# Value projections ahead of the loop, first q and k stored without waiting for other rows, pairing of steps from step 4 on

## The reference

```
def attn(x, w_q, w_k, w_v, w_o):                    # 16 heads of 16
    q, k, v = x @ w_q.T, x @ w_k.T, x @ w_v.T       # split into heads
    scores = einsum('bqhd,bkhd->bhqk', q, k) * 0.25
    out = einsum('bhqk,bkhd->bqhd', softmax(scores), v)
    return out.reshape(B, S, D) @ w_o.T

def ffn(x, W_r, W_k, W_v, mu_r, mu_k):              # xp: x moved down by one row
    xr, xk = mu_r * x + (1 - mu_r) * xp, mu_k * x + (1 - mu_k) * xp
    return sigmoid(xr @ W_r.T) * (relu(xk @ W_k.T) ** 2 @ W_v.T)

x = x + layernorm(attn(layernorm(x)))
x = x + layernorm(ffn(layernorm(x)))
```

## Time and profile before

| | |
|---|---|
| median of 3 runs | 1214.42 us (1211.47 to 1215.19) |
| the profiled execution | 1209.24 us, its span 1207.1 us |
| PE busy | 1185.9 us, 98% of the span |
| ACT busy | 1055.6 us, 87% |
| DVE busy | 781.3 us, 65% |
| POOL busy | 274.3 us, 23% |
| granted PE clock | 0.9 or more in each of 40 slices |

### The profile page before, as it was taken

One profiled execution on the slowest core, in us unless ns is written; L12 is line 12 of the kernel. 1 busy time (PEld: TensorE's weight loads), 2 busy tenths in 40 slices (PEclk: granted clock), 3 DMA queues, 4 the chain that ended last, 5 costly groups with the idle time before them and its releaser, 6 DMA issues.

```text
span 1207.1 us, 25766 instructions
## 1 busy us (share of the span) xinstructions
PE 1185.9 (98%) x10588; PEld 652.0 (54%) x10588; DVE 781.3 (65%) x1833; ACT 1055.6 (87%) x1409; POOL 274.3 (23%) x350
## 2 busy tenths in 40 slices
PE   7999999999999999999999999999999999999997
PEld 5544555455555555555555555555555555535455
DVE  7553757758575766847667585766768466464646
ACT  4789898899989999898998989899898999999882
POOL 2000223222221322222222222223222122222132
PEclk9999999999999999999999999999999999999999
DMA  4457563317622185214934166321871139400100
GB/s 162 116 127 192 116 131 79 115 53 140 113 66 89 55 176 105 62 63 113 152 71 123 39 135 117 81 89 54 152 130 47 43 98 160 97 1 19 53 14 23
DMA packets 61943, 113.77 MB, mean 94 GB/s; under 512 B 6528, under 2 KB 31360, under 8 KB 61632
## 3 DMA queue, kind: packets, MB, share of 16 engines
q1 hardware_dynamic: 61504, 110.65, 40.7%
q10 hardware_dynamic: 288, 1.05, 0.3%
HBM read 69.47 MB, written 41.94 MB: 92 GB/s over the span
## 4 chain that ended last, share of the span: by engine, by line
PE 95%; ACT 2%; DVE 2%; DMA 1%; issue 0%; POOL 0%; POOLq 0%; SPq 0%; DVEq 0%
PE O L542 39%; PE M L524 28%; PE M L481 23%; PE M L423 3%; ACT PT L721 1%; PE M L451 1%; PE M L652 1%; DMA xA<-x_dram 1%; DVE sth L926 0%; PE M L645 0%; PE M L629 0%; DVE QS L889 0%; ACT QS L749 0%; PE M L587 0%; DVE xB L1066 0%
## 5 line engine op out<-in xcount | busy, mean ns | idle before, releaser
L721 ACT ACTIVATE PT<-M 128x1024 f32<-128x1024 f32 x1274 | 1000.7, 866 | 110.6 <-PE M L524 99.9
L524 PE MATMUL M<-QS,KS 50*128 50x512 f32 x2048 | 499.9, 419 | 7.9 <-ACT PT L721 7.9
L542 PE MATMUL O<-PT,V 128*17 128x512 f32 x4096 | 490.3, 595 | 0.0
L524 PEld LDWEIGHTS M<-QS,KS 50*128 50x128 f32 x2048 | 221.9, 185 | 264.0 <-ACT PT L721 234.7
L542 PEld LDWEIGHTS O<-PT,V 128*17 128x17 f32 x4096 | 93.3, 96 | 228.6 <-issue 209.5
L481 PE MATMUL M<-xnT,WH 64*128 64x512 f32 x496 | 143.2, 406 | 0.0
L1332 POOL TENSOR_SCALAR veh<-mvh 128x2 f32<-128x2 f32 x90 | 19.9, 221 | 399.6 <-DVE mvh L929 399.6
L1173 DVE SCALAR_TENSOR_TENSOR A<-Z,M 128x512 f32<-128x512 f32 x30 | 20.6, 687 | 110.5 <-PE M L481 110.5
L481 PE MATMUL M<-WH,xnT 64*128 64x256 f32 x480 | 84.6, 284 | 0.0
L481 PE MATMUL M<-WH,C 64*128 64x256 f32 x480 | 84.0, 285 | 0.0
L481 PE MATMUL M<-WH,B 64*128 64x256 f32 x480 | 83.9, 285 | 0.0
(11 more groups left out here) (164 smaller groups left out, 1698.1 us busy)
## 6 DMA issues: line engine op xcount, KB each, us to landing
scr<-p SPq DMA_DIRECT2D x124, 256.0 KB
QS<-scr SPq DMA_DIRECT2D x56, 256.0 KB, 6.8
KS<-scr SPq DMA_DIRECT2D x56, 256.0 KB, 9.5
QS<-scr SPq DMA_DIRECT2D x70, 128.0 KB, 5.6
KS<-scr SPq DMA_DIRECT2D x68, 128.0 KB, 7.8
xA<-x_dram SPq DMA_DIRECT2D x16, 512.0 KB, 7.0
xB<-x_dram SPq DMA_DIRECT2D x16, 512.0 KB, 7.6
out_dram<-xB SPq DMA_DIRECT2D x15, 512.0 KB, 3.2
```

Source lines behind the costliest of these rows:

```text
L524: e.matmul(PM[bank[i, j]], KS[qd][rows, pair, kt * 128:kt * 128 + 128], QS[qd][rows, pair, hf * 512:hf * 512 + 512], start=True, stop=True) \
L542: ins = e.matmul(PO[32 * j:32 * j + 17, :], V[b % 2][:, kt, 4 * qd + j, :], PT[i % 3][:, j, :], start=(kt == 0), stop=(kt == 7))
L721: e.activation(PT[i % 3][:, j:k + 1, :], PB[:, at:at + len(numbers), :], ACT.Exp, scale=SCALE) \
```

## The change

- **Tables.** PAIRED is 4. FIRST has no V2 and V3; K00, K10, Q10, K01 begin at steps 0 to 3, K11 at 4, Q01 and Q11 at 14 and 16; T1 and the pieces of batch 1 behind it come two steps later. ALONE_IN is gone: V1, V2, V3 and Q00 stand in ALONE. The values of the first unit so stand wholly ahead of the loop.
- **Banks.** V0, T11, V1, V2 and V3 go through two of the scores banks (IN_SCORES); the scores of step 0 wait for V3's and V2's bank there.
- **Start.** The first 512 rows of x come in two transfers, one on SP, one ahead of the others on ACT's queue. PE makes all six idle products first, then T00 and T01, then the Gram products. DVE takes the second statistics after the first norm and lowering, and norms the second rows in one go; the addition of epsilon moves from POOL to DVE, here and for all batches. POOL makes the lower parts of wv, wq and wk in DVE's place. ACT makes the upper copies of E01 and E11.
- **Stored q and k.** The order is Q00 (ahead of the loop), K00, K10, Q10, K01, K11, Q01, Q11. For batch 0 `store` waits for no spread. The spreads of quads 1 to 3 have other steps and other groupings.

```diff
-PAIRED = 12
+PAIRED = 4
-FIRST = {2: "V2", 3: "K01", 4: "V3", 5: "Q10", 6: "K10", 7: "K11", 8: "Q01", 9: "Q11", 12: "T0", 18: "T1", 20: "Q00",
-         22: "K00", 24: "Q01", 26: "K01"}
+FIRST = {0: "K00", 1: "K10", 2: "Q10", 3: "K01", 4: "K11", 12: "T0", 14: "Q01", 16: "Q11", 20: "T1", 22: "Q00",
+         24: "K00", 26: "Q01", 28: "K01"}
-ALONE = ("T00", "T01", "D00", "E00", "T10", "D10", "T11", "E10", "V0", "E01", "E11")
-ALONE_IN = {0: ("V1", "Q00"), 1: ("K00",)}
+ALONE = ("T00", "T01", "D00", "E00", "D10", "V0", "E10", "T10", "T11", "V1", "E01", "E11", "Q00", "V2", "V3")
+IN_SCORES = {"V0": 2, "T11": 3, "V1": 2, "V2": 3, "V3": 2}
-SENT = ("Q00", "K00", "K01", "Q10", "K10", "K11", "Q01", "Q11")
+SENT = ("Q00", "K00", "K01", "K10", "Q10", "K01", "K11", "Q01", "Q11")
-FIRST_SPREADS = {2: [(1, (0, 1), (0,))], 6: [(1, (1,), (1,))], 7: [(2, (0, 1), (0,))], 8: [(2, (1,), (1,))],
-                 10: [(3, (0, 1), (0,)), (3, (1,), (1,))], 16: [(qd, (0,), (1,)) for qd in range(4)]}
+FIRST_SPREADS = {2: [(1, (0,), (0,))], 3: [(1, (1,), (0,))], 6: [(1, (1,), (1,))], 7: [(2, (1,), (0,)), (2, (0,), (0,))],
+                 10: [(3, (0, 1), (0,))], 11: [(2, (1,), (1,)), (3, (1,), (1,))],
+                 20: [(qd, (0,), (1,)) for qd in range(4)]}
...
-        at = [i] if i < 9 else [i, i + 1]
-        then = [i + 1] if i < 8 else [i + 2] if i == 9 else [j for j in range(at[-1] + 1, i + 12) if j < STEPS and not turns[j]][:2]
+        at = [i] if i < PAIRED else [i, i + 1]
+        then = [i + 1] if i < PAIRED else [j for j in range(at[-1] + 1, i + 12) if j < STEPS and not turns[j]][:2]
...
+            e.dma_start(xA[:, 2:4, :], x[0, 256:512, :].rearrange("(t p) c -> p t c", p=128)) \
+                .then_inc(*up(xa0_in, ("xA0", 0), by=16))
             e.dma_start(wide, wpack[:, 3588:4612]).then_inc(*up(wide_in, ("wide_in",), by=16))
...
-                    p.wait_ge((("hi", "lo")[j], piece), *lately[mt])
+                    p.wait_ge((("hi", "lo")[j], piece), *(lately[mt] if b else ()))
```

More of the change, by code:

```diff
@@ L144, in left @@
         return of[piece], ("bank", piece)
+    in_scores = {}
     for word in ALONE:
[L147 to L150, removed]
+        if word in IN_SCORES:
+            k = IN_SCORES[word]
+            of[word, 0], freed[word, 0] = k, in_scores.get(k)
+            in_scores[k] = left((word, 0))[1]
+        else:
             take((word, 0), free)
             free.append(left((word, 0)))
+    for i in range(PAIRED):
         half = HALVES[i][0]
@@ L155, in banks @@
             take(half[0], free)
-        if i not in ALONE_IN:
-            free += [left(piece) for piece, _ in ENDS[i]]
+        free += [left(piece) for piece, _ in ENDS[i]]
     for i in range(PAIRED + 1):
@@ L180, in banks @@
         if not TURNS[i]:
-            free += [left(piece) for piece, _ in ENDS[i + 1]]
+            free += [left(piece) for piece, _ in ENDS[i] + ENDS[i + 1]]
     u = UNITS - 1
@@ L662, in tensor @@
                             .then_inc(*up(pe_wrote, ("gram", n, t, k)))
-            warm(2)
-            alone(("T00", 0))
-            alone(("T01", 0))
-            warm(1)
-            alone(("D00", 0))
-            alone(("E00", 0))
+            for word in ("D00", "E00", "D10"):
+                alone((word, 0))
             p.wait_ge(("gram_sums",))
             e.matmul(m0[:, 0:2], mask[:, :], gsm[:, 0:2], start=True, stop=True).then_inc(*up(pe_wrote, ("by_head",)))
-            alone(("T10", 0))
-            alone(("D10", 0))
+            for word in ("V0", "E10", "T10", "T11"):
+                alone((word, 0))
             p.wait_ge(("below",), ("half_set",))
@@ L675, in tensor @@
                 .then_inc(*up(pe_wrote, ("how_many",)))
-            for word in ("T11", "E10", "V0", "E01", "E11"):
+            for word in ALONE[9:]:
                 alone((word, 0))
@@ L788, in scalar @@
             first("T01")
-            parted("wv")
-            for word in ("D00", "E00", "T10", "D10", "T11", "E10"):
+            for w in ("wv", "wq", "wk"):
+                parted(w)
+            for word in ALONE[2:]:
                 first(word)
-            parted("wq")
-            parted("wk")
-            first("V0")
             exponentials(0, 0, 1)
@@ L1212, in vector @@
                 .then_inc(*note(("below",)))
-            after_DE(("E00", 0), 0)
             after_T(("T10", 0), 0, True)
+            after_T(("T11", 0), 0, True)
+            after_DE(("D10", 0), 0)
+            after_DE(("E10", 0), 0)
+            after_DE(("E01", 0), 0)
             p.wait_ge(("how_many",))
```

122 lines of the change are left out of this document (58 added, 64 removed).

## The result

The forecast was 1212.0 us, 2.4 us less than before and within what can be told from no change. Measured side by side, in 20 executions each, the changed kernel has a median of **1215.30 us** (1209.93 to 1219.49) and the kernel before 1211.04 us; the ratio, taken from all executions and not from the two medians, is **1.0027, with a 95% interval of 1.0016 to 1.0039**. The change makes the kernel slower, by 0.3%. The forecast of 1212.0 was built on a median of 3 executions (1214.42), which lies 3.4 us above that of the 20. So it is the difference that has to be compared: -2.4 us forecast, +4.3 between the medians.

The account below looks back on a forecast made before the run. TensorE, busy 98%, was taken to bound the kernel. Terms 4.2 - 2.1 - 5.4 + 0.1 + 0.5 + 0.3 = -2.4 us on the 1207.1 span, carried in proportion to the 1214.42 median, gave 1212.0; range 1208.8 to 1216.5.

Parts of the forecast that it names:

- The wait before E01: Ahead of the loop: TensorE waits 2.05 us for VectorE to lower D10, whose bank E01 takes.
- Steps 0 to 3: Loop's first four steps, each with one projection slot: 13.95 us instead of 16.07, 2.1 us gained.
- The paired periods: Two loop steps at a time cost about 4.39 us, empty or with one piece; steps 4 to 11 gain 5.4.
- D00: Product ahead of the loop: starts at 12.3 us, 2.4 earlier, with transposes at 9.3.
- The 0.5 for K11's wait: First paired period: K11 waits for Q10's bank, held up by K00's store; 0.5 us lost, bounds 0 and 2.2.
- The values of steps 14 and 15: In the loop: these values products start near 71.9 us instead of 74.33.
- norm 1.35: Start of the kernel: VectorE's norm takes 1.35 us in the chain from x's arrival to the transposes.
- no wait before E10: Ahead of the loop: no wait counted for E10's products on TensorE, their last result 7.75 us after D00's start.
- rival 4: Start: TensorE's clock falls while idle after warm-up, transposes and Gram products take 2.95 more; +0.6 us, 1215.0, chance 0.05.
- landing at 20.0: Quad 1's k spread, issued 16.0 us into the loop, lands 4.0 later; TensorE asks at 19.4, 0.3 lost.
- Rival 3: Quad 1's k path: stores and spreads bind, both loop waits growing to 7.7 us; +4.5 us, 1218.9, chance 0.13.
- its two waits: In the loop: waits at K11 and for quad 1's k spread; slower by over 0.3% once together past 6.8 us.

Follow-up runs that it names:

- run with GpSimd's wait: Changed kernel with GpSimd waiting for the norm of rows 512 to 1023 before making the lower parts of wq and wk: 1215.21 us, ratio to before 1.0030.
- the run with two powers: Kernel before, with TensorE's scores of steps 28 and 29 waiting for two extra GpSimd powers whose result nothing uses: 1215.36 us, ratio 1.0030.
- the run with idle products: Changed kernel with unused TensorE products in both long waits, before E01 and before the scores of step 8: 1212.43 us, ratio to before 1.0005.
- the three edits: Changed kernel with quad 1's k and q spreads a step earlier, D10 lowered before T10 and T11, GpSimd's lower parts after the norm: 1208.12 us, ratio 0.9966.
- the two edits ahead of it: Changed kernel with GpSimd's lower parts of wq and wk after the second rows' norm, and D10 lowered before T10 and T11: together 1212.73 us, ratio 1.0011.

## Why the prediction was wrong, step by step

**Right.** The wait before E01 was put at 2.05 and was 2.02, ended by VectorE as foreseen. Steps 0 to 3 were put at 13.95 and took 13.83, from 34.91 to the next scores at 48.74. The paired periods behind step 9 take 4.37 to 4.60. Behind steps 14 and 15 the difference to before grows by 0.4 only. D00 was put at 12.3 and started at 12.28, but this is in part luck: x came at 4.30 instead of 4.8, the transposes started at 9.64 instead of 9.3, behind the idle products (they end at 9.34) and a constant (mu) that landed late, and from the transposes to D00 it took 2.64 instead of 3.04.

**Not as forecast, at little cost.** The 0.5 for K11's wait hardly came (0.2 at most). VectorE copies Q10 at 47.91, as soon as PE has made it, so K00's store was out of the buffer earlier than the 13.95 behind the loop's start that were forecast, and K11's first products start at 49.37, directly behind the lowering of Q10 (48.63 to 49.32). The 0.55 in the row at 50.41 is a wait of scores for ScalarE. Even so the first paired period takes 5.60 (48.74 to 54.34), 0.7 more than the 4.39 and 0.5 forecast for it.

**Wrong, in three steps.** The values of steps 14 and 15 were put at 71.9 and started at 80.13. The 8.2 us are:

| step of the prediction | forecast | measured | us |
|---|---|---|---|
| "norm 1.35", the second rows' norm in one go | no wait before E10 | wait of 1.51 | +1.5 |
| rival 4, the clock, ahead of the loop | 2.93 for E01 and E11 | 4.58 | +1.65 |
| small differences in other places, the first paired period among them | | | -0.1 |
| "landing at 20.0", the k spread of quad 1 | 0.3 | wait of 2.08, and ACT's lag behind it | +2.0 |
| rival 4, the clock, in the loop | 1.91 for 16 values products | 3.61, and its neighbours | +3.2 |

The last two add up to the 18.66 us from the row at 52.49 to that at 71.15, against three periods of 4.39 and the 0.3 of the forecast. The profiled run with GpSimd's wait has such a wait, of 2.63, and no fall of the clock behind it, and needs 16.06 for the same stretch (49.23 to 65.29): 2.9 above the three periods for a wait of 2.63. With 2.08 in its place that is 2.3, of which 0.3 was forecast, and what is left, 3.2, is the clock. The two kernels with idle products at step 8, whose clock stays at 1.00 there, bear this out: in their profiled executions they need 16.15 and 16.16 with a stop that is 0.6 longer than the wait in after.

The first step failed in adding a duration from a place where GpSimd was idle to a place where it is not: the change itself moved GpSimd's lower parts there. The duration was right, the neighbour was forgotten.

The second step failed by the choice of the row. The 4.0 us from issue to landing were read at 43.56 in the earlier trace rows, where the spread stands alone on the queue and takes 1.71 to issue. Between the rows quoted there stand others that were not used, in the same view of before:

```profile
54.10 2.82 SPq L1459 DMA_DIRECT2D KS<-scr  x4
...
58.97 3.17 SPq L1459 DMA_DIRECT2D QS<-scr  x4
```

At most 0.7 us behind the transfer before it a spread takes 2.8 to 3.2 to issue, as it did in after (2.99). That alone is 1.3 us of the 2.5 by which the spread landed late (22.5 behind the loop's start, not 20.0). The rest lies behind the last issue; it was not taken apart. Rival 3 named this place as the one where the change turns slower. By the prediction its two waits had to pass 6.8 us together before the change turned slower: there was one, of 2.08, and it tipped.

It tipped by the third step, rival 4, the clock, which had a chance of 0.05 and stood in the sum at nothing. Two things were wrong in it. First, it was looked for at one gap only, behind the warm-up, and this gap was never there: the change makes all six idle products first, the prediction counted on the end of the three of before (5.76), and in after they run from 1.44 to 9.34, so that PE waited 0.30. That its time, 1215.0, is close to the measured one is luck. The wait of 2.05 before E01, which the prediction brought itself, stood there as a plain cost, without being asked the same question. Second, the tail was read rightly, and too much was concluded from it. PE stopped near 1200.8, and in shorter windows the clock is 1.00 to 1204, 0.98 to 1206 and 0.50 behind it. But this is one end of work, in one execution, and no measure of when the clock can fall between two bursts. Waits of 2.0 to 2.3 us among busy stretches did bring the falls, and the run with two powers shows that one such wait is enough (3.7 us). The Trainium skill, "TensorE: Matmul & The Clock Gate", section "HAM oscillation — how this bites in real kernels", warns of waits between bursts that send the array back to half clock: on the direction it was right, and the conclusion from the tail was wrong.

**The size.** The measured 1215.30 lies inside the forecast's range (1208.8 to 1216.5), but only by its base, which was 3.4 us too high; counted from 1211.04 the same range would end at 1213.1. Without the clock's two falls the change comes out at no difference (the run with idle products, 1.0005): the forecast's -2.4 plus 1.5 for the norm, 2.0 for the spread and 0.6 by which the idle products prolong the stop is +1.7, and the measured difference of its median is +1.4. That fits with the structure of the change being worth about what the prediction gave it, though no run takes the pairing or the earlier pieces apart. With the three edits, which take away the blocked norm, the wait at D10's bank and the late spread, the kernel gains 2.5 us on before.

**Open.** Which of several waits the clock answers to is not settled. It fell behind two waits of some 0.3 and 0.4 us in the run with idle products ahead of E01 only and in that with all three edits. It did not fall behind a wait of 2.63 in the profiled run with GpSimd's wait, though 11 of the 12 executions of that kernel had a mean clock of 0.997 or less. Executions of before, whose waits on PE from 8 us on are 1.1 us at most up to step 12, differ in the same way: those with a mean clock of 0.999 or more have a span of 1207.7 (32 executions), those of 0.997 1210.3 (20), those below 1213.8 (13). Its profiled execution, 1207.1 at 1.00, was one of the best, so the rows of before showed no fall at all.

## What to carry over

Where TensorE bounds a kernel, price a new wait of 2 us at about twice its length (4.3 us for 2.26 in the one place where it was tried alone) and ask of each, not only of the largest, what the clock does behind it; if the wait can't be removed, idle products in it take back the larger part. Take a duration from a row with the same neighbours: what GpSimd does beside it for an instruction of VectorE, what is queued ahead of it for a transfer. A gain ahead of a loop is worth only what the next late operand leaves of it, so mend the wait in the loop first: alone it took back 4.4 us, the two edits ahead of it 0.1 and 0.7, and 2.6 as a pair. And where the time of one kernel differs from execution to execution by its clock, one profiled execution does not show whether it suffers: look at the mean clock of many.

## What was not expected of the hardware

- One wait of 2.26 us of TensorE in a run at full load was followed by about 7 us at 1.2 GHz and moved the median by 3.7 us against a wait of 1.17 us, which was followed by no fall. Executions of one and the same kernel differ in this: 1.4 us of span for each us of lost clock, (1 - clock) x span, by a line through 97 executions of before.
- A norm of 128x256 in fp32 on VectorE takes 0.40 us alone and 1.28 to 1.37 beside a subtraction of 1.30 to 1.33 us on GpSimd, whose own length hardly changed (1.29 alone).
- A spread of four transfers takes 1.71 us to issue on a free queue of SyncE and 2.8 to 3.4 when it goes at most 0.7 us behind another transfer, and the k spread of quad 1 was readable 6.5 to 7.7 us after the start of its issue, against 4.0 for one that stood alone.
- x in two halves, on SyncE's and ScalarE's queue, was there 2.0 us earlier than in one transfer (4.30 and 6.31), with the same bytes to move. The halving and the second queue were not tried apart.
